# Layer 0 of a two-layer convolution network: every second group's v as a 1x1 product on TensorE and nine taps on ScalarE and VectorE

## The reference, cut to what matters

```python
hidden = einsum('bchw,oc->bohw', x, w_hidden) + b_hidden      # 64 -> 384
hidden = conv(hidden, w_dw, 3x3 depthwise, 'SAME') + b_dw
q, k, v = split(hidden, 3, axis=1)                            # 128 each
out = irfft2(rfft2(patches(q)) * rfft2(patches(k)))           # patches of 8x8
out = (out - mean) / sqrt(var + 1e-05) * ln_w + ln_b          # over channels
return einsum('bchw,oc->bohw', v * out, w_proj) + b_proj      # 128 -> 64
```

## Time and profile before

| what | us |
|---|---|
| median of 3 runs | 9394.1 (9379.17 to 9394.48) |
| the profiled execution | 9387.86 |
| its span in the profile | 9385.9 |
| layer 0's loop, from its start to its last matmuls | some 225 to 6787 |
| TensorE, VectorE, ScalarE, POOL busy | 9042.0, 6029.8, 6408.4, 4911.1 |

### The profile page before, as it was taken

The page is one execution under the profiler, slowest core; times in us unless marked ns, Lnnn a source line. Parts: engine busy times, 40 slices in busy tenths (PEclk is TensorE's granted clock), DMA queues, the critical chain, the costliest instruction groups (busy, mean ns, idle before and its releaser), DMA issues. The chain is left out here.

```text
span 9385.9 us, 168801 instructions
## 1 busy us (share of the span) xinstructions
PE 9042.0 (96%) x58884; PEld 5002.5 (53%) x58884; DVE 6029.8 (64%) x7793; ACT 6408.4 (68%) x8676; POOL 4911.1 (52%) x2751
## 2 busy tenths in 40 slices
PE   0999999999999999999999999999987999999999
PEld 0666666666666666666666666666532333333333
DVE  4555555555555555555555555555566999999999
ACT  0676676666666666766766676676604888888888
POOL 1444444344444434444443444434305999999999
PEclk9999999999999999999999999999998999999999
DMA  6222222222222222222221212122195444444444
GB/s 142 52 49 64 49 59 59 56 59 49 64 51 58 60 54 59 49 64 49 59 59 42 50 40 50 40 50 50 34 237 121 118 118 120 120 120 119 118 119 118
DMA packets 618105, 715.18 MB, mean 76 GB/s; under 512 B 44230, under 2 KB 577196, under 8 KB 594200
## 3 DMA queue, kind: packets, MB, share of 16 engines
q1 hardware_dynamic: 618008, 713.88, 31.6%
HBM read 549.02 MB, written 164.70 MB: 76 GB/s over the span
## 5 line engine op out<-in xcount | busy, mean ns | idle before, releaser
L573 PE MATMUL banks<-w_hi,hi_lo 128*128 128x256 f16 x18432 | 2351.3, 273 | 51.7 <-DVE hi_lo L837 51.7
L573 PEld LDWEIGHTS banks<-w_hi,hi_lo 128*128 128x128 f16 x18432 | 1784.3, 98 | 456.9 <-ACT qk L716 204.5
L531 POOL TENSOR_TENSOR u_im<-q_im,k_swap 128x512 f32<-128x512 f32 x512 | 727.3, 1421 | 2103.3 <-ACT q_im L734 2031.1
L716 ACT ACTIVATE qk<-banks,inv_wscale 128x512 f32<-128x512 f32 x1024 | 704.2, 688 | 1504.6 <-PE banks L573 1491.5
L1324 POOL TENSOR_TENSOR part_sum<-part_sum,prod 128x1024 f32<-128x1024 f32 x660 | 1561.3, 2366 | 53.4 <-POOL part_sum L1324 0.4
L1353 PE MATMUL banks<-z,conv_w 128*128 128x512 f32 x3128 | 1575.1, 619 | 0.0
L846 DVE TENSOR_TENSOR u<-q_re,banks 128x512 f32<-128x512 f32 x512 | 350.9, 685 | 1483.2 <-ACT q_re L736 1475.6
L521 POOL TENSOR_TENSOR hl_all<-xn,hi_all 64x1280 f16<-64x1280 f32 x258 | 793.2, 3075 | 584.7 <-ACT hi_all L709 533.7
L590 PE MATMUL banks<-hi_lo,w_hi 128*128 128x512 f16 x4608 | 1084.1, 380 | 10.0 <-DVE tmp L915 10.0
L534 POOL TENSOR_TENSOR u<-u,u_im 128x512 f32<-128x512 f32 x512 | 651.0, 1272 | 690.7 <-DVE u L846 675.9
L573 PE MATMUL banks<-w_lo_pair,hi_pair 128*128 128x256 f16 x6144 | 1006.0, 273 | 0.0
(11 more groups left out here) (217 smaller groups left out, 15959.4 us busy)
## 6 DMA issues: line engine op xcount, KB each, us to landing
xr<-in_x_dram SPq DMA_DIRECT2D x258, 640.0 KB, 9.0
xb<-y_scratch SPq DMA_DIRECT2D x268, 320.0 KB, 4.5
xa<-y_scratch SPq DMA_DIRECT2D x268, 256.0 KB, 5.0
x_res<-in_x_dram SPq DMA_DIRECT2D x258, 256.0 KB, 3.8
out_dram<-res SPq DMA_DIRECT2D x258, 256.0 KB, 3.2
y_scratch<-ys SPq DMA_DIRECT2D x256, 256.0 KB, 3.8
yc<-y_scratch SPq DMA_DIRECT2D x256, 256.0 KB, 5.4
xs<-in_x_dram SPq DMA_DIRECT2D x92, 512.0 KB, 7.1
```

The lines of the kernel that those rows point to most:

```text
L531: nc.gpsimd.tensor_tensor(u_im[:], q_im[:], k_swap[:], ALU.mult).then_inc(u_made, 1)
L573: r = pe.matmul(out, px, w, start=n == 0, stop=n == 13)
L716: act.activation(qk[:, 2 * h:2 * h + 2, :], b_qk[h][:].rearrange("p (t c) -> p t c", t=2), ACT.Copy, scale=inv_wscale[:, 0:1]).then_inc(qk ...
```

## The change

The v of odd groups is no longer made by conv_v. A new `hidden` makes the 1x1 product of 66 columns x 10 rows (the group's 64 x 8 with a border) in ten matmuls, into 660 columns across banks 4 and 5; ScalarE's middle_tap writes v_s as the middle tap with bias and scale, and VectorE's taps adds the other eight in place, two ahead of means and six behind it. b_y moves from bank 7 to bank 5, b_o to 6, b_var to 7.

TensorE's forward of an odd group moves into tile 0 of the next group, its inverses move from a group's end to behind tile 0 of the group after, the projection behind the third tile; it also waits for the taps. On ScalarE, square goes between the two qk copies, and high_parts ahead of the second. On VectorE, high_below goes behind product, x_chunk from k == 5 to the end of k == 4; next_variance and averages go one group later. The setup makes the weights of the hidden product, scaled separately. `run` splits off the first iteration of each loop.

```diff
+        hid_hi = sb("hid_hi", [P, P], F16)
...
+        tap_w = sb("tap_w", [P, 11])
...
+                    for n, tap in enumerate((7, 1)):
+                        sp.dma_start(row_sel[p0 + tap:p0 + tap + 1, 2 * n + part:2 * n + part + 1],
+                                     A["b_sel"][p0 + tap:p0 + tap + 1, part:part + 1]).then_inc(v_loaded, 16)
...
+                then(v.tensor_copy(hid_w[:], wh[:, KQ:KV]))
+                then(v.tensor_copy(hid_b[:], bh[:, KQ:KV]))
+                then(v.scalar_tensor_tensor(hid_tmp[:], hid_w[:], -1.0, hid_w[:], ALU.mult, ALU.max))
+                then(v.tensor_reduce(wmax[:, 8:9], hid_tmp[:], AX_X, ALU.max))
...
-            b_qk, b_f, b_v, b_o, b_var, b_y = (bank[0], bank[1]), (bank[2], bank[3]), bank[4], bank[5], bank[6], bank[7]
+            b_qk, b_f, b_v, b_y, b_o, b_var = (bank[0], bank[1]), (bank[2], bank[3]), bank[4], bank[5], bank[6], bank[7]
...
+            hidden_v = bank_pair[2][:].rearrange("p a n -> p (a n)")[:, 182:842].rearrange("p (c r) -> p c r", r=R + 2)
+            by_column = lambda t: t.rearrange("p (c r) -> p c r", r=R)
...
-                for n in range(1, NI):
-                    with eng.Fori(start, n * IT - 2) as i:
-                        body(i, False, True, None, False)
-                    with eng.Fori(n * IT - 2, n * IT - 1) as i:
-                        body(i, False, n < NI - 1, n, False)
+                for n in range(1, NI + 1):
+                    end = n * IT - 2 if n < NI else NB - 1
+                    for i0, i1 in ((start, start + 1), (start + 1, end)):
+                        if i0 < i1:
+                            with eng.Fori(i0, i1) as i:
+                                body(i, False, n < NI, None, False)
...
+                def hidden(b, cg):
+
+                    for h in range(2):
+                        cols = slice(GCOL * cg + 33 * h, GCOL * cg + 33 * h + 33)
+                        out = hidden_v[:, 33 * h:33 * h + 33]
+                        pe.matmul(out[:, :, 0:R], hid_hi[:], hi_lo[b][0][:, cols, :], start=True, stop=False)
+                        pe.matmul(out[:, :, R:R + 2], hid_hi[:], hi_lo[b][2][:, cols, R - 2:R], start=False, stop=False)
+                        pe.matmul(out[:, :, 2:R + 2], hid_lo[:], hi_ind[b][:, cols, :], start=False, stop=False)
+                        pe.matmul(out[:, :, 0:2], hid_lo_top[:], hi_pair[b][:, cols, 0:2], start=False, stop=False)
+                        last = pe.matmul(out[:, :, 0:2], hid_bias_top[:], hi_ind[b][:, cols, 0:2], start=False, stop=True)
+                    last.then_inc(v_hidden, 1)
+
                 def project(i, k):
...
+                    if not (k and isinstance(i, int) and i == NB):
+                        pe.wait_ge(v_tapped, i * 32 + 8 * (k // 2))
...
+                def transform_ready(i, k, any_before):
+
+                    pe.wait_ge(qk_copied, i * 16 + (2 * k + 2))
+                    if any_before:
+                        pe.wait_ge(k_read, i * 8 + k)
+                        pe.wait_ge(q_copied, i * 8 + k)
...
-                            made = conv(b, b_qk[t // 2][:, KQ * (t % 2):KQ * (t % 2) + KQ], 4 * cg + t)
+                            late = t == 0 and k % 2 == 0 and not (first and k == 0)
+                            made = conv(b, b_qk[t // 2][:, KQ * (t % 2):KQ * (t % 2) + KQ], 4 * cg + t,
+                                        (lambda: transform_ready(i, k - 1, True)) if late else None)
                             if t % 2:
                                 made.then_inc(qk_conv, 1)
-                            if t == 1 and k % 2 == 0 and not (first and k < 4):
+                            if late:
+                                forward()
+                            if t == 0 and not (first and k < 2):
+                                inverse(i, k - 1, not (first and k == 2))
+                            if t == 1 and k % 2:
+                                pe.wait_ge(v_copied, i * 4 + (k + 1) // 2)
+                                if not (first and k < 5):
+                                    pe.wait_ge(fin_read, i * 4 + (k - 3) // 2)
+                                hidden(b, cg)
+                            if t == 2 and k % 2 == 0 and not (first and k < 4):
                                 project(i, k)
...
-                        conv_v(b, cg, transform_ready).then_inc(v_conv, 1)
-                        forward()
-                        if not (first and k == 0):
-                            inverse(i, k, not (first and k == 1))
+                        if k % 2 == 0:
                             if not (first and k == 0):
-                                pe.wait_ge(k_read, i * 8 + k)
-                                pe.wait_ge(q_copied, i * 8 + k)
...
+                                pe.wait_ge(v_tapped, i * 32 + 8 * (k // 2))
+                            if image is not None and k == 4:
+                                averages(image)
+                            conv_v(b, cg, lambda: transform_ready(i, k, not (first and k == 0))).then_inc(v_conv, 1)
+                            forward()
...
+                def middle_tap(i, k, ring_used):
+
+                    act.wait_ge(v_hidden, i * 4 + (k + 1) // 2)
+                    if ring_used:
+                        act.wait_ge(fin_done, i * 4 + (k - 4) // 2 + 1)
+                    act.activation(by_column(v_s[k % 4][:]), hidden_v[:, 1:GCOL + 1, 1:R + 1], ACT.Identity,
+                                   bias=tap_w[:, 10:11], scale=tap_w[:, 4:5]).then_inc(v_begun, 1)
...
+                def taps(i, k, n0, n1):
+
+                    v_out = by_column(v_s[k % 4][:])
+                    for n in range(n0, n1):
+                        t = n if n < 4 else n + 1
+                        dr, dc = TAPS[t]
+                        if n == 0:
+                            v.wait_ge(v_begun, i * 4 + (k + 1) // 2)
+                        else:
+                            v.wait_ge(v_tapped, i * 32 + (8 * ((k - 1) // 2) + n))
+                        v.scalar_tensor_tensor(v_out, hidden_v[:, 1 + dc:GCOL + 1 + dc, 1 + dr:R + 1 + dr], tap_w[:, t:t + 1],
+                                               v_out, ALU.mult, ALU.add).then_inc(v_tapped, 1)
...
+                        if not (first and k == 0):
+                            product(i, k, not (first and k == 1))
                         if k % 4 == 2:
                             high_below(s, b)
-                        if not (first and k == 0):
-                            product(i, k, not (first and k == 1))
                         if not (first and k < 2):
                             times_v(i, k, not (first and k < 6))
+                        if k % 2:
+                            taps(i, k, 0, 2)
                         if not (first and k == 0):
                             means(i, k)
+                        if k % 2:
+                            taps(i, k, 2, 8)
+                        if stats and k == 4:
+                            x_chunk(i)
```

More of the change, by code:

```diff
@@ new lines, in _ @@
+                then(v.memset(hid_lo_top[:], 0.0))
+                then(v.tensor_tensor(hid_lo[0:C], hid_w[0:C], hid_hi[0:C], ALU.subtract))
+                then(v.tensor_copy(hid_lo_top[0:C], hid_lo[0:C]))
+                then(v.tensor_scalar(hid_b[:], hid_b[:], wmax[:, 8:9], None, ALU.mult))
+                then(v.tensor_copy(hid_b_hi[:], hid_b[:]))
+                then(v.tensor_tensor(hid_b[:], hid_b[:], hid_b_hi[:], ALU.subtract))
+                then(v.memset(hid_bias_top[:], 0.0))
+                for n, to in enumerate((hid_lo, hid_bias_top)):
+                    then(v.tensor_scalar(hid_tmp[:], hid_b[:], row_sel[:, 2 * n + 1:2 * n + 2], None, ALU.mult))
+                    then(v.scalar_tensor_tensor(to[C:P], hid_b_hi[C:P], row_sel[C:P, 2 * n:2 * n + 1], hid_tmp[C:P],
+                                                ALU.mult, ALU.add))
@@ L218, in _ @@
+                then(v.tensor_scalar(wmax[:, 2:3], wmax[:, 6:7], 1e-30, None, ALU.max))
                 then(v.tensor_scalar(inv_wscale[:], wmax[:, 2:3], 1.0 / WSCALE, None, ALU.mult))
@@ L320, in _ @@
                 pe.wait_ge(asked, 1)
-                pe.matmul(bank[0][:, 0:2], pair_avg[:], tmp[:, 0:2, :].rearrange("p a i -> p (a i)"),
-                          start=True, stop=True).then_inc(answered, 1)
+                for q in range(4):
+                    for a in range(2):
+                        made = pe.matmul(bank[0][32 * q:32 * q + 32, a:a + 1], pair_avg[:, 32 * q:32 * q + 32], tmp[:, a, :],
+                                         start=True, stop=True)
+                made.then_inc(answered, 1)
         y_stats = sb("y_stats", [P, NS * 2, 6])
@@ L385, in build_program @@
             v_copied = tsem("v_copied")
+            v_hidden = tsem("v_hidden")
+            v_begun = tsem("v_begun")
+            v_tapped = tsem("v_tapped")
             k_freq = tsem("k_freq")
@@ L565, in _, with conv @@
             def _(pe):
```

(23 more changed lines are left out.)

59 lines of the change are left out of this document (39 added, 20 removed).

## The result

The changed kernel takes 9168.4 us (median of 4 runs, 9159.0 to 9173.1) against 9391.4 for the kernel before: ratio 0.976, 95% interval 0.975 to 0.978, 223 us less. The forecast was 9187.

What follows compares the result with a forecast made beforehand. TensorE's queue was taken to bound layer 0; -517 (TensorE's gain) + 287 (new wait) + 23 (once) = -207 from the profiled 9387.9 gives 9181, and the median 6 higher: 9187 us, range 8895 to 9320.

Steps and rivals of the forecast that it cites:

- TensorE's gain: Per pair of groups in layer 0: 3.12 us of conv_v less 1.0 hidden product and 0.1 type change, 517 us in all.
- The chain: Through VectorE and POOL, group 1's forward to the next strip's group 0 inverse: 26.81 us against TensorE's 24.57.
- high_below in front of POOL's add: Between product and times_v: POOL's add starts 1.57 us behind product's start; without this order the second term would be 2.27.
- the late inverse's wait: TensorE at the inverse in a strip's group 0, waiting for POOL's less_mean: 2.24 us in 128 strips, 287 us.
- L994 beside the low part: Finish's sum on VectorE, L880 before the change: 3.46 us instead of 1.09, waiting for POOL's second low part; it stays.
- rival 1: No wait appears and TensorE stays the bound, as when L880 is served ahead of the low part: 8900 us, 13%.
- Taps: VectorE's eight per odd group: 0.74 us each at a pitch of 0.77, 6.2 us per pair.
- Rival 3: VectorE becomes the bound through the taps' short-run bank reads; slower from 1.17 us a tap, 9557 at 1.30; 8%.
- The clock: TensorE's granted clock falls in the new waits, tiles at half rate for some us per strip: about 9570 us, 2%.
- rival 4: TensorE's clock falls in the new waits: 3 us in each of 128 strips, about 9570 us, 2%.
- Once-costs: Outside the repeating strips: setup 8 us, averages for the next image 13, tail 2, sum 23 us.
- The extra loop bodies: Splitting off each loop's first iteration costs nothing, as no boundary shows in TensorE's waits.

Runs made afterwards that it cites:

- e1: The changed kernel with VectorE's high_below put back ahead of product in the third group of a strip: 9079.4 us, ratio 0.967 to the kernel before.
- e2: The changed kernel with POOL's two low parts one behind the other at the third group's start: 8869.4 us, ratio 0.944 to the kernel before.
- e4: The changed kernel with the last six taps of odd groups working on 8 of 512 elements: 9165.2 us, ratio 0.976 to the kernel before.
- e10: The changed kernel with the loops of before, their first iterations not split off: 9296.3 us, ratio 0.990 to the kernel before.
- e12: The kernel before with the changed kernel's loops, the first iteration of each split off: 9543.3 us, ratio 1.016 to the kernel before.
- e11: The changed kernel with one unused f16 matmul of 0.22 us ahead of the late inverse's wait: 9097.8 us, ratio 0.969 to the kernel before.
- e3: The changed kernel with eight unused f16 matmuls in the late inverse's wait: 9319.1 us, ratio 0.992 to the kernel before.
- e7: The changed kernel with two unused f32 matmuls in the late inverse's wait: 9357.5 us, ratio 0.997 to the kernel before.

## Why the prediction was right, by its steps

- *TensorE's gain*, 2.02 a pair: measured 25.57 - 23.28 = 2.29, so 586 us instead of 517. The term that was mis-sized most is the hidden product. Its ten matmuls run from 3008.88 to the next tile at 3009.68, 0.80 instead of 1.0: here ten loads don't cost 98 ns each one behind the other. What is left of the 2.29, 3.12 - 0.80 - 2.29 = 0.03, is the 0.1 for the extra change between product types. The Trainium skill (TensorE: Matmul & The Clock Gate, back-to-back issue gap) gives by its formula an estimate of 0.63 for the ten, but calls it one for a matmul by itself that counts too little for short matmuls with loads of their own; the 0.80 agrees with that.
- *The chain*, 26.81: measured 26.43. Its pieces, from the rows above: 4.93 to product (4.94 forecast), 2.71 to means (2.85), 14.10 to group 3's product (14.17), 2.64 (2.74), 2.0 (2.01), 0.05 (0.1). The walk through one strip held to 0.4 us. The wait was to be 2.24; the strip gives 48.70 - 2 x 23.28 = 2.14 for it and the one in front of the last tile together, 274 us for 287. The forecast didn't see that second wait. It is high_below's move that makes the stacks late, since e1 takes it away.
- *high_below in front of POOL's add*: held in its price, not in its form: the add doesn't start 1.57 behind the product but 0.83, and takes 0.57 longer, near the 0.72 in which the two overlap. e1 gives the price of the order, 89 us with its share of the clock's, but by the stacks' wait and the clock and hardly by the late inverse's wait. The Trainium skill (SBUF — State Buffer, shared port pair) has the loser blocked for the whole instruction; the trace agrees: L994 ends 0.97 behind the low part's end (3028.91 and 3027.94), nearly its own 1.08 alone, and the add 1.13 behind high_below's, nearly its own 1.27.
- *L994 beside the low part*: it was named as the point on which rival 1 hangs (3.58 here, 3.46 before). e2 took it away and came to 8869; rival 1's 8900 less 69 for TensorE's larger gain would be 8831, and the 0.3 us a strip that e2 still waits make up the 38 between them.
- *Taps*: 749 ns, pitch 0.76. Rival 3 (from 1.17 on) is out, by the row and by e4.
- *The clock* (rival 4, 2%): the step that failed. It does fall in the new wait, in a third of the strips, for 71 us. The price was overrated (1.7 us in 42 strips, not 3 us in 128), but the chance was set far too low, from one thousand us with a 3.3 us wait and a mean clock of 1.00. The kernel before has three such waits of 3.3 us, and the clock fell behind the two others:

```profile
3335.00:3342.00 7.00, 5.86 (x14) 1.94 (x14) 1.02 (x3) 1.62 (x1) 0.69 (x1) 0.51 0.04 10
4980.00:4984.00 4.00, 4.00 (x11) 1.47 (x12) 0.00 (x0) 0.43 (x1) 0.00 (x0) 0.57 0.01 4
```

  A mean over 1000 us wouldn't have told: 4000 to 5000, with the second of these falls in it, also reads 1.00. Windows of a few us around each wait would have.
- *Once-costs*: setup 7 (8); averages 11 (13), as the strips at the images' ends and the ones behind these give it without the 5 us already counted for the clock. The wait itself is 5.6 us each and not 7.5; the rest is mostly slow clock, which now falls behind all three; the drain 0 (2).
- *The extra loop bodies: nothing.* No boundary shows, as forecast, but it isn't a neutral part. Without it this code takes 9296 (e10), and with it before takes 9543 (e12). Of the 223 us gained, 128 hang on where the loops came to lie. That the term came out as nothing is luck: the forecast had no reason for it that e10 and e12 bear out.

Sum: -586 + 274 + 71 + 7 + 11 = -223, and the profiled spans differ by 9385.9 - 9164.7 = 221. That 9187 came so near owes something to luck: the cheap hidden product and shorter wait (82 us) against a clock that wasn't in the sum (71).

## What to carry to other kernels

When work leaves the bounding engine, walk one period of the next chain in order of time, with the meetings on VectorE's and POOL's port in it: here two neighbours in the wrong order (L994 and the low part) cost 299 us with the clock's share, more than the change brought. A wait on TensorE of 1.8 us can cost its own length again in clock, and cutting it to 1.4 with one cheap matmul took that cost away here. Read the clock right behind each wait, since a mean over 1000 us hides a fall. Before a small change's time is believed, compare the instruction queue's packets and look for waits with no releaser, since a loop that moved can hide or feign 100 us or more.

## What the runs showed of the hardware that was not expected

- The granted clock falls to 0.53 for about 3 us behind 42 of 72 waits of 1.83 to 1.84 us, behind none of 55 of 1.76 in the same run, behind 13 of 127 of 1.6 to 1.84 in e1, and behind none of 1.43 to 1.51 with a 0.22 us matmul ahead of them (e11). In the kernel before it fell behind two of three waits of 3.3 us.
- TensorE can stand for 2 to 10 us in each pass of a loop for its instructions, in one copy of a loop and not in another of the same body. Such a loop brings 9 packets of 16 KB on the instruction queue in every pass, the others none behind their first (e3, e7, e10, e12).
- A VectorE sum of 1.08 us takes 3.58 beside POOL's low part, while taps that read a bank keep their 0.75 beside the same operation, and products that read a bank their 0.67 to 0.69 beside POOL's add.
